# A twelve-layer decoder on one core: another layer's running sums in layer 0's second pass, values behind the scores, biases without products

## The reference

```python
# layer 0 (L0a): causal attention, 16 heads of 16 features; kernel class SmallHeads
x = _layernorm(x + _L0_attn_ref(x, w_attn, b_attn, w_proj, b_proj))

# layers 3 (L1a) and 9 (L3a): 16 query heads of 128 features, one shared key/value head; class WideHeads, kv "shared"
q = (x @ Wq + bq).reshape(B, S, H, D)
k = x @ Wk + bk
v = x @ Wv + bv
scores = jnp.einsum('bnhd,bmd->bnhm', q, k) * scale
attn = jax.nn.softmax(scores, axis=-1)
out = jnp.einsum('bnhm,bmd->bnhd', attn, v).reshape(B, S, H * D)
return out @ Wo + bo

# layer 5 (L1f): weights rounded to three values by the mean of their absolute values; class BitLinear
scale = 1.0 / jnp.maximum(jnp.mean(jnp.abs(w)), EPS)
q = jnp.clip(jnp.round(w * scale), -1.0, 1.0) / scale
```

## Time and profile before

| | value |
|---|---|
| profiled execution, its span | 2365.69 us, 2364.1 us |
| PE busy | 1892.7 us (80%) |
| DVE busy | 1375.7 us (58%) |
| ACT busy | 894.0 us (38%) |
| POOL busy | 314.5 us (13%) |
| chain that ended last | PE 57%, DVE 27%, issue 7%, ACT 5% |
| mean granted TensorE clock | 0.858 |
| largest groups on the chain | L1322 7%, L1249 7%, L1312 7%, L936 6%, L1283 6%; L1658 1% |

### The profile page before, as it was taken

One profiled execution on the slowest core, in us unless ns is written; L12 is line 12 of the kernel. 1 busy time (PEld: TensorE's weight loads), 2 busy tenths in 40 slices (PEclk: granted clock), 3 DMA queues, 4 the chain that ended last, 5 costly groups with the idle time before them and its releaser, 6 DMA issues.

```text
span 2364.1 us, 29032 instructions
## 1 busy us (share of the span) xinstructions
PE 1892.7 (80%) x10398; PEld 1305.4 (55%) x10398; DVE 1375.7 (58%) x2535; ACT 894.0 (38%) x2121; POOL 314.5 (13%) x265
## 2 busy tenths in 40 slices
PE   5664768747735777689998979979999999999895
PEld 3432444414412445566666748865666766667652
DVE  3359956869988461666666128883666235554214
ACT  1335512145422116366665036433555034443000
POOL 2303520005500105111111000000000000000100
PEclk9985568765557889899999999997999999999876
DMA  4010020010010210000001010000001000000000
GB/s 115 8 37 0 1 60 0 5 56 0 1 45 1 39 48 2 14 14 16 13 13 56 8 73 1 1 1 7 9 11 49 1 18 12 13 30 1 36 1 18
DMA packets 25742, 49.18 MB, mean 21 GB/s; under 512 B 6262, under 2 KB 19603, under 8 KB 24092
## 3 DMA queue, kind: packets, MB, share of 16 engines
q1 hardware_dynamic: 25644, 47.85, 6.7%
...
## 4 chain that ended last, share of the span: by engine, by line
PE 57%; DVE 27%; issue 7%; ACT 5%; SPq 2%; DMA 1%; POOL 1%; DVEq 0%; ACTq 0%; POOLq 0%; PEldq 0%
PE banks L1322 7%; PE banks L1249 7%; PE banks L1312 7%; DVE big L936 6%; PE banks L1283 6%; PE banks L1304 3%; DVE big L556 3%; PE banks L1564 2%; PE banks L1974 2%; PE banks L1953 2%; PE banks L463 2%; PE banks L474 2%; ACT big L2080 2%; DVE big L1658 1%; PE banks L1270 1%
## 5 line engine op out<-in xcount | busy, mean ns | idle before, releaser
L1399 DVE COPY arena<-banks 128x512 f32<-128x512 f32 x196 | 135.3, 690 | 259.2 <-PE banks L1304 255.4
L1312 PE MATMUL banks<-arena,big 128*128 128x256 f32 x784 | 217.5, 400 | 9.0 <-DVE arena L1399 8.9
L1283 PE MATMUL banks<-big 128*128 128x256 f32 x784 | 209.6, 391 | 1.6 <-ACT big L1436 1.6
L222 POOL TENSOR_TENSOR ln_rstd<-ln_var_eps,neg_half 128x2 f32<-128x2 f32 x48 | 37.8, 787 | 1249.8 <-DVE ln_var_eps L210 1249.8
L1462 ACT ACTIVATE arena<-banks,arena 128x256 f32<-128x256 f32 x392 | 193.3, 501 | 19.0 <-DVE arena L1354 15.7
L1249 PE MATMUL banks<-x_feat,arena 128*128 128x512 f32 x392 | 178.2, 598 | 1.2 <-ACT big L1446 1.2
L1480 ACT ACTIVATE big<-banks 128x256 f32 (+1 forms) x196 | 75.3, 384 | 274.6 <-PE banks L1312 274.6
L1312 PEld LDWEIGHTS banks<-arena,big 128*128 128x128 f32 x784 | 139.6, 191 | 66.6 <-DVE arena L1399 52.5
L1322 PE MATMUL banks<-arena,big 128*128 128x256 f32 x784 | 174.3, 382 | 1.9 <-ACT big L1480 1.9
L1322 PEld LDWEIGHTS banks<-arena,big 128*128 128x128 f32 x784 | 147.5, 190 | 27.5 <-issue 4.6
L1354 DVE TENSOR_REDUCE arena<-banks 128x2 f32<-128x512 f32 x196 | 134.4, 686 | 41.2 <-PE banks L1283 41.1
...
## 6 DMA issues: line engine op xcount, KB each, us to landing
...
```

The costliest lines, as they stand in the source:

```text
L1283: last = mm(ps[:, h * SEQ:(h + 1) * SEQ], q[:, b * SEQ + h * P:b * SEQ + (h + 1) * P], k[:, b * SEQ:(b + 1) * SEQ], start=not self.mask, s ...
L1312: last = mm(slot, self.v[:, 2 * b + kc, :], self.probs_t[:, u % 2, kc, :], start=(kc == 0), stop=(kc == 1))
L1399: v.tensor_copy(self.probs_t[:, u % 2].rearrange("p a b -> p (a b)"), B[4 + u % 2][:]).then_inc(self.turn_read, 1)
```

## The change

It has three parts.

1. RunningSums is no longer a block. An object of that name belongs to layer 0's SmallHeads. The 16 x 16384 words lie in two pieces, 2624 words in the other arena and 13760 at the end of `big`, over the stage buffer that the projections used; SP loads both once the stage has been moved out, ahead of the DMAs of the maxima. ScalarE takes the absolute values in four parts (656 + 3440 words), one behind each `read_max`. VectorE scans 2624 words ahead of the first copy of the second pass and 860 words behind each of its 16 copies, each piece starting from the last value of the one before.
2. WideHeads "shared" makes k and q first, then the scores of steps 0 and 1, then v; TensorE then waits for the reads of v (`proj_read` 6) ahead of its loop. ScalarE reads in the same order, v behind the exponentials of both steps.
3. Neither bias is a product now. v's bias becomes a column of 128 partitions, added by ScalarE as it copies the output (Identity with a bias in place of Copy). The output bias is loaded to all 128 partitions, and VectorE adds it to x_tok at the layer's start, once the tiles have been turned (`xt_psum`).

The diff, without unchanged parts:

```diff
@@ -242,6 +243,57 @@
+ASIDE_FROM = 7104
+class RunningSums:
+    SIZE = 1024 * D // LANES
+    def __init__(self, e, rooms, units):
+        self.e = e
+        self.loaded, self.absolute = e.lanes_loaded, e.lanes_absolute
+        self.pieces, at = [], 0
+        for room in rooms:
+            n = min(room.shape[1], self.SIZE - at)
+            self.pieces.append((at, n, room[0:LANES, 0:n]))
+            at += n
+        assert at == self.SIZE
+        first, rest = self.pieces[0], self.pieces[1]
+        step = -(-rest[1] // units)
+        self.chunks = [first[2]] + [rest[2][:, i:min(i + step, rest[1])] for i in range(0, rest[1], step)]
+    def load(self, sp):
+        for at, n, room in self.pieces:
+            sp.dma_start(room, self.e.dram["L1f_lanes"][:, at:at + n]).then_inc(self.loaded, 16)
+    def make_absolute(self, act, part, parts):
+        act.wait_ge(self.loaded, 32)
+        for at, n, room in self.pieces:
+            step = n // parts
+            cols = room[:, part * step:(part + 1) * step if part < parts - 1 else n]
+            self.e.nc.scalar.activation(cols, cols, ACT.Abs).then_inc(self.absolute, 1)
+    def scan(self, dve, n):
+        e, ch, v = self.e, self.e.dve_chain, self.e.nc.vector
+        w = self.chunks[n]
+        if n == 0:
+            dve.wait_ge(self.absolute, 2 * 4)
+        before = self.chunks[n - 1] if n else None
+        start = before[:, before.shape[1] - 1:before.shape[1]] if n else 0.0
+        ch.link(dve, v.tensor_tensor_scan(w, w, w, start, ALU.add, ALU.max))
+        if n == len(self.chunks) - 1:
+            v.tensor_copy(e.lane_sums[:, 0:1], w[:, w.shape[1] - 1:w.shape[1]]).then_inc(e.lanes_summed, 1)
@@ -278,10 +330,12 @@
         self.v = big.take(TILES, 16, 32)
-        self.stage = big.take(2, 2, TOKENS)
         self.out_first = big.take(TOKENS)
...
         self.max_rows = big.take(groups, P, parts=32)
+        past = big.at
+        self.stage = big.take(2, 2, TOKENS)
+        self.aside = RunningSums(e, [e.arenas[1 - l % 2].tensor[:, ASIDE_FROM:e.arenas[1 - l % 2].words], big.tensor[:, past:big.words]], self.units) if l == 0 else None
         self.att = k_words[:, 0:TILES * 64 * groups].rearrange("p (t d) -> p t d", t=TILES)
@@ -348,6 +402,10 @@
                         sp.dma_start(dst, self.stage[row:row + w, s, blk, :]).then_inc(self.moved[blk], 16)
+        if self.aside:
+            for blk in range(2):
+                sp.wait_ge(self.moved[blk], 16 * (8 * self.per_block + 4 * (blk == 0)))
+            self.aside.load(sp)
         for g in range(self.groups):
@@ -566,9 +624,13 @@
                 self.beside.vector_slot(dve, n)
+            if u == 0 and self.aside:
+                self.aside.scan(dve, 0)
             dve.wait_ge(self.summed, u + 1)
...
                                   e.banks[:, slot:slot + 2, 3 * P:4 * P]).then_inc(self.sum_read, 1)
+            if self.aside:
+                self.aside.scan(dve, u + 1)
@@ -632,11 +694,15 @@
                 read_max(u // 4 - 1)
+                if self.aside:
+                    self.aside.make_absolute(act, u // 4 - 1, 4)
             for n in self.first_slots(u):
...
         read_max(G - 1)
+        if self.aside:
+            self.aside.make_absolute(act, 3, 4)
         for u in range(self.units):
@@ -1080,9 +1147,8 @@
-    def __init__(self, e, l, arena, name, heads, kv, scale, mask=False, wo_heads=16, aside=None):
+    def __init__(self, e, l, arena, name, heads, kv, scale, mask=False, wo_heads=16):
         self.e, self.l, self.name, self.heads, self.kv, self.scale, self.mask = e, l, name, heads, kv, scale, mask
-        self.aside = aside
         self.unroll = {"shared": 2, "pair": 4, "each": 2}[kv] if heads > 1 else 1
@@ -1095,7 +1161,7 @@
             self.q_bias = a.take(2)
-            self.q_b, self.k_b, self.v_b, self.o_b = a.take(heads), a.take(1), a.take(DH, parts=1), a.take(D, parts=1)
+            self.q_b, self.k_b, self.v_b, self.o_b = a.take(heads), a.take(1), a.take(1), a.take(D)
         if wo_heads > heads:
@@ -1128,6 +1194,8 @@
+    first = {"k": 0, "q": 2, "v": 4}
@@ -1175,7 +1243,7 @@
             loads += [(self.kv_w, d[n + "_kv_w"]), (self.q_b, d[n + "_q_b"]), (self.k_b, d[n + "_k_b"]),
-                      (self.v_b, d[n + "_v_b"]), (self.o_b, d[n + "_o_b"])]
+                      (self.v_b, d[n + "_v_b"].rearrange("a f -> f a")), (self.o_b, d[n + "_o_b"].rearrange("a f -> (a f)").partition_broadcast(P))]
         if self.kv == "each":
@@ -1264,8 +1332,7 @@
                                 for c in range(CH):
-                                    mm(out, e.x_feat[:, c, tok], self.kv_w[:, c, DH:2 * DH], start=(c == 0), stop=False)
-                                last = mm(out, e.ones[0:1, :], self.v_b, start=False, stop=True)
+                                    last = mm(out, e.x_feat[:, c, tok], self.kv_w[:, c, DH:2 * DH], start=(c == 0), stop=(c == CH - 1))
                             else:
@@ -1274,7 +1341,7 @@
-                pe.wait_ge(self.proj_read, self.place(i, r, "k_turn" if self.kv == "each" else "q") + 2)
+                pe.wait_ge(self.proj_read, self.first["q"] + 2 if self.kv == "shared" and u == 0 else self.place(i, r, "k_turn" if self.kv == "each" else "q") + 2)
             ps, q, k = B[2 + u % 2], self.q[:, r % 2], self.k[:, self.kv_parity(r)]
@@ -1285,10 +1352,14 @@
         if self.kv == "shared":
-            produce(0, 0, ["v", "k"], first={"v": 0, "k": 2})
-        produce(0, 0, self.takes(0))
+            produce(0, 0, ["k", "q"], first=self.first)
+        else:
+            produce(0, 0, self.takes(0))
         score(0, 0)
         score(0, 1)
+        if self.kv == "shared":
+            produce(0, 0, ["v"], first=self.first)
+            pe.wait_ge(self.proj_read, 6)
         if self.kv == "each":
@@ -1319,9 +1390,7 @@
             for h in range(self.heads):
-                last = mm(e.y_bank(t), self.out[:, h, t * P:(t + 1) * P], wo[h], start=(h == 0), stop=(h == self.heads - 1 and not self.bias))
-            if self.bias:
-                last = mm(e.y_bank(t), e.ones[0:1, :], self.o_b, start=False, stop=True)
+                last = mm(e.y_bank(t), self.out[:, h, t * P:(t + 1) * P], wo[h], start=(h == 0), stop=(h == self.heads - 1))
             if t % 2:
@@ -1342,10 +1411,11 @@
             v.tensor_tensor(self.v, self.v, bcast(self.mask_col, 2, DH), ALU.mult).then_inc(self.v_masked, 1)
+        if self.bias:
+            dve.wait_ge(e.xt_psum, 4 * self.l)
+            ch.link(dve, v.tensor_tensor(e.x_tok[:], e.x_tok[:], bcast(self.o_b, 1, TILES), ALU.add))
         if self.wo_heads > self.heads:
             ch.link(dve, v.tensor_reduce(self.wo_sum, self.wo.rearrange("p h n -> p n h"), AX.X, ALU.add))
-        if self.aside:
-            self.aside.scan(dve)
@@ -1464,10 +1534,13 @@
         if self.kv == "shared":
-            read(0, 0, ["v", "k"], first={"v": 0, "k": 2})
-        read(0, 0, self.takes(0))
+            read(0, 0, ["k", "q"], first=self.first)
+        else:
+            read(0, 0, self.takes(0))
         exps(0, 0)
         exps(0, 1)
+        if self.kv == "shared":
+            read(0, 0, ["v"], first=self.first)
         if self.kv == "each":
@@ -1477,7 +1550,7 @@
                 slot = B[6 + u % 2][:, 0:SEQ]
-                a(self.out[:, bass.ds(self.unroll * i + r, 1), b * SEQ:(b + 1) * SEQ].rearrange("p h t -> p (h t)"), slot, ACT.Copy).then_inc(self.out_read, 1)
+                a(self.out[:, bass.ds(self.unroll * i + r, 1), b * SEQ:(b + 1) * SEQ].rearrange("p h t -> p (h t)"), slot, *((ACT.Identity, self.v_b) if self.bias else (ACT.Copy,))).then_inc(self.out_read, 1)
@@ -1626,46 +1699,6 @@
-class RunningSums:
-    def __init__(self, e, l):
-        self.e, self.l = e, l
-        self.size = HIDDEN * D // LANES
-        self.w = e.big.tensor[0:LANES, e.big.words - self.size:e.big.words]
-        self.loaded, self.absolute = e.sem("lanes_loaded"), e.sem("lanes_absolute")
-    def sync(self, sp):
-        e, l = self.e, self.l
-        if l >= 1:
-            sp.wait_ge(e.xt_ready, 4 * l)
-        sp.dma_start(self.w, e.dram["L1f_lanes"]).then_inc(self.loaded, 16)
-    def scalar(self, act):
-        act.wait_ge(self.loaded, 16)
-        self.e.nc.scalar.activation(self.w, self.w, ACT.Abs).then_inc(self.absolute, 1)
-    def scan(self, dve):
-        e, ch, v = self.e, self.e.dve_chain, self.e.nc.vector
-        dve.wait_ge(self.absolute, 1)
-        ch.link(dve, v.tensor_tensor_scan(self.w, self.w, self.w, 0.0, ALU.add, ALU.max))
-        v.tensor_copy(e.lane_sums[:, 0:1], self.w[:, self.size - 1:self.size]).then_inc(e.lanes_summed, 1)
-    def vector(self, dve):
-        pass
-    def tensor(self, pe):
-        pass
-    def gpsimd(self, pool):
-        pass
@@ -2314,20 +2347,17 @@
             11: lambda l: Thought(e, l, e.arenas[l % 2], "L3f"),
-            3: lambda l: WideHeads(e, l, e.arenas[l % 2], "L1a", 1, "shared", 1 / DH, aside=lanes[0] if lanes else None),
```

(6 more changed lines are left out.)

4 lines of the change are left out of this document (3 added, 1 removed).

## The result

The changed kernel took 2343.74 us (median of 4 runs, 2342.78 to 2344.62), the kernel before 2373.86 (4 runs, 2368.13 to 2379.76): a ratio of 0.9879, 95% interval 0.985 to 0.9908, 30.1 us less. Timed once more beside the last experiments it was 0.9884 (0.9858 to 0.991). The forecast was 2338 in a range of 2317 to 2353, faster: the time is 5.7 us above the point and inside the range. The forecast started from a median of 2368.63 for the kernel before; with one more run of it the median is 5.2 higher. Profile against profile the gain is smaller: 2365.69 to 2342.78, 22.9 us, where the sum said 30.3.

A forecast was written before the change was run, and what follows sets the result against it. One core runs twelve layers as a chain of waits with hardly any overlap; VectorE's running sum holds layer 3. Layer 3 −29.7, layer 9 −17.8, layer 0 +17.2 sum to −30.3: 2335.4, or 2338 on the median's scale, range 2317 to 2353.

The forecast's parts named there:

- the first turn: First transposes of the probabilities: layer 3 at 428.5 instead of 454.15, −25.6 us; layer 9 at 1618.7 instead of 1631.40, −12.7.
- the first steps: TensorE's steps after the first turn, no longer slowed by the lower clock after idling: layer 3 −1.7 us, layer 9 −1.5.
- the tail: End of the layer without output-bias products, 0.62 us for each token tile: layer 3 −2.4, layer 9 −5.0.
- keys and queries: Layers 3 and 9: time from the start of the keys to the scores, taken as 10.6 us from layer 9's 10.55.
- the rest of the steps: Layer 9: output copies with a bias take 0.09 us more each, one a head counts, +1.4; bounds 0 and 5.8.
- the step on the two loads: Layer 0, first pass: loads ahead of the DMAs of the maxima priced at nothing, given 7.3 us of slack.
- The second step, scan 0 holding the masks: Layer 0, start of second pass: scan 0 holds back the first masks, first copy at 90.6 instead of 87.59, +3.0 us.
- the collisions: Layer 0, second pass: scans and GpSimd masks exclude each other, 3.33 us a period instead of 2.38, +14.2 over 15 periods.
- The last scan: Layer 0, after the last copy: the scan lies beside TensorE's 5.4 us of transposes.
- The rival "lower clock": TensorE at half rate in layer 0's second pass, +25 us, and in layers 3 and 9: 2385, 2%; layer 0 alone 3%.
- a fall of the clock in the second pass: Layer 0: sign that the forecast is wrong, if TensorE's clock falls in the second pass.

The follow-up runs named there:

- The run with that edit alone: Kernel before, with only the output bias added to x_tok by VectorE in layers 3 and 9 and its products gone; profiled 2375.58 us, layer 9 300.68.
- The run with Abs later: Changed kernel with the Abs in three parts behind the second, third and fourth read of the maxima, none behind the first; layer 0 161.85 us.
- the one-input sum: Changed kernel with scan 0 early, each later scan replaced by a VectorE sum over 1800 words with one SBUF input; layer 0 148.84 us.
- the run with the scan left in layer 3: Changed kernel's new order and biases without products, but running sum left on VectorE in layer 3; profiled 2356.04 us, layer 0 148.29.

## Why the prediction was right, and where it was off

The mechanisms in layers 3 and 9 were right. Layer 3: the first turn comes 19.12 us after LayerNorm's last power (435.41 to 454.53) instead of 45.97, −26.9 for a forecast of −25.6; the first steps −1.7 as forecast; the tail −2.8 for −2.4. What was mis-sized there and in layer 9 is keys and queries: 9.43 instead of 10.55, since the first eight rows take 5.22 where they stood behind 15 us of small products and took 6.34. Why the upper level comes sooner now isn't shown. In layer 9: first turn −13.6 for −12.7, first step −1.5 as forecast, the rest of the steps +1.4 for +1.4, as the longer output copies would have it. The tail is −6.4 for −5.0: the bias product was priced by its two rows, 0.62, but a tile of 32 rows took 7.73 with it and 6.91 without, and the tail as a whole, from the first product with the output weights, fell from 63.97 to 57.60, 0.80 a tile. The run with that edit alone has the same tail; its layer 9 gained only 5.96 because its first turn came 0.3 later and its steps took 0.1 longer.

Layer 0 is the term that failed by size: +27.6 for +17.2. It failed first in the step on the two loads, "so I price them at nothing". The forecast bounded what waiting for them would cost by ScalarE's slack of 7.3 us. The slack was right, the landing time was not looked at: the larger load, 860 KB in 16 rows, took 11.1 us from issue to landing. ScalarE waited 9.36 for it, the Abs of 3.6 came behind, the second read of the maxima was 5.9 late, and the lower level behind TensorE's idle time made it 7.2. The run with Abs later shows it: 5.9 of it back at the first copy. The second step, scan 0 holding the masks, was forecast at +3.0 and is +3.2 (85.77 to 98.00 against 78.55 to 87.59). The third, the collisions, was forecast at 3.33 a period, +14.2, and is 3.53 (53.00 for 15), +17.3. That scan and mask hold each other up is shown by the stretched masks and the one-input sum; but by the copies only six periods are at the upper level, three of 2.53 and three of 3.83 with a collision in them, 3.18 on average where the forecast had 3.33. Nine are at the lower level, wholly or in their first part, 3.55 to 3.81. A period at that level is 3.74 without any scan (the run with the scan left in layer 3), so a scan costs at most 0.07 there and the clock the rest: of the 17.3 us these nine are 12.5, the six with collisions 4.8. The last scan was free, as forecast: 13.1 us from the last copy to GpSimd's first power, 13.2 before. 7.2 + 3.2 + 17.3 = 27.7.

The rival "lower clock" thus took place in layer 0 alone, in nine of 15 periods, and cost less than its 25 us, because a period at the lower level hides the collisions, which the forecast had counted beside it. The forecast had itself named a fall of the clock in the second pass as a sign that it was wrong, and by that sign its account of layer 0 was: it has the collisions and lacks the level that they bring down.

That the median came down by 30.1, as forecast, and the profiles by 22.9, is partly fortune: layer 0 missed by 10.4 us, and layers 3 and 9 made up 3.9 of it. The median's larger fall comes from the kernel before. Its profiled execution was the fastest seen of it (2365.69; its other runs 2368 to 2380), with the shortest layer 0 of the three profiles of that code (143.28, 146.63, 148.29) and the shortest layer 6. Layer 6, which holds the same kind of loop and no edit that acts, took 218.8 to 231.1 in the thirteen profiles, and layer 11 132.6 to 132.9 in twelve of them, 129.8 in the changed kernel's first. Layer 6 goes with the clock: 218.8 at a granted clock of 0.90, 223.2 at 0.87, 231.1 at 0.84, and nearly all of the 12.3 us between the first and the last are in TensorE's busy time (154.1 and 166.3). Layer 11 fits this (0.67 in the short one, 0.65 in the others). What brings the clock to one or the other there was not tried.
